# A linear attention on one core: queries kept as hi and lo halves in one tile, two phase passes for three

## The chip, the cores and the metric

The kernel runs on one core of one Trainium2 chip. The metric is the device time of one execution in microseconds (us). Three executions before the change took 1333.11, 1334.69 and 1338.66 us; their median, 1334.69 us, is the time before.

## The reference, cut to what matters

The program is one layer of a graph network over 1250 nodes of 1024 features: a first layer norm, a graph attention over 20000 edges, a linear attention, a feed-forward block and a quantised one. The change touches the linear attention alone:

```
p  = einsum('blhd,dm->blhm', x, proj_mat) / math.sqrt(D_HEAD)      # for queries and for keys
qp = kp = concatenate([cos(p), sin(p)], axis=-1) / math.sqrt(D_KMAP)
kv   = einsum('blhm,blhd->bhmd', kp, v)
attn = einsum('blhm,bhmd->blhd', qp, kv)
```

There are 16 heads of 64 features, and proj_mat is 64x128. The sines and cosines need phases p of nearly full float32 accuracy.

## The kernel before

TensorE works here on fp32r, a shortened float32. To keep accuracy every operand is split into hi (the value written as fp32r) and lo (the value less hi, again fp32r), and a product is three matmuls that add up in PSUM: lo times hi, hi times lo, hi times hi.

`linear_attention` takes two heads at a time, a pair: 8 pairs, a loop of 7 iterations and a last pair written out. The features of the pair lie on the 128 partitions (head 0 on 0 to 63, head 1 on 64 to 127) and the 1250 nodes along the columns, in three thirds of 418, 416 and 416 columns. A pair has, on TensorE (`block.tensor`, `pair`):

- products for values, keys and queries (`product`, L1414): three runs of 24 matmuls each, one run per third. ScalarE adds the bias and writes hi (`keep_run`, L1179); VectorE waits for that and writes lo (`keep_run`, L1306). Both read the product from PSUM.
- ten steps, k = 0 to 9. Steps 0 to 4 are for keys (`key_phases`, L1455, then `accumulate_kv`, L1477: six matmuls), steps 5 to 9 for queries, 250 nodes each (`query_phases`, L1465, then `attend`, L1489: twelve matmuls).

In every step the phases go from PSUM through three instructions of VectorE (`phases`: L1327 whole turns, L1329 the part of a turn, L1332 minus its absolute value, the only one of the three that reads SBUF alone), then through two sines and a copy to hi on ScalarE (`cos_sin`: L1201, L1203, L1214). The difference to lo is made by GpSimd in even steps (`keep_lo`, L1140) and by VectorE in odd ones (`keep_lo`, L1336). `accumulate_kv` and `attend` wait for that lo. The step buffers are double (k % 2).

The queries are held as q_hi and q_lo, each 128 partitions by 1250. proj_hi and proj_lo are 128 x 2 x 128: block h holds proj_mat in the 64 partitions of head h and zeros in the other 64, so that one matmul over all 128 partitions gives the phases of head h alone. Half of the array's rows multiply by zero.

The order on each engine is written out by hand in four functions called `pair`. What matters here is the order on the two elementwise engines, in which the query thirds stand first:

```
ScalarE: query third 0, weights' hi (keys), cos_sin 2, query third 1, weights' hi (values), cos_sin 3, query third 2, cos_sin 4, ...
VectorE: query third 0, keep_lo 1, phases 2, query third 1, phases 3, query third 2, keep_lo 3, phases 4, phases 5, ...
GpSimd:  keep_lo 0, weights' lo (keys), keep_lo 2, weights' lo (values), keep_lo 4, weights' lo (queries), keep_lo 6, keep_lo 8
TensorE: query run 0, accumulate 0, key phases 2, query run 1, accumulate 1, key phases 3, query run 2, accumulate 2, key phases 4,
         value run 0, accumulate 3, query phases 5, value run 1, accumulate 4, query phases 6, value run 2 with the transposes of kv, ...
```

The weights' hi and lo (L1171 on ScalarE, L1136 on GpSimd) are for the next pair, whose weights SyncE loads after it has issued the store of the pair before. The last pair has no next one: no value or key runs lie between its steps there, and ScalarE and VectorE split the weights of the following stage instead (L1221, L1340).

Of the kernel before, what the change touches and what calls it, by code (L numbers as in the profile page):

```python
# [5 lines left out]
ALU = mybir.AluOpType  # L6
ACT = mybir.ActivationFunctionType
AX = mybir.AxisListType
F32 = mybir.dt.float32
F32R = mybir.dt.float32r  # L10
# [5 lines left out]
N, D = 1250, 1024  # L16
# [10 lines left out]
HEADS, DH, KMAP = 16, 64, 128  # L27
# [13 lines left out]
def f32(ap):  # L41

    return ap.bitcast(F32)
# [933 lines left out]
VALUE, KEY, QUERY = 0, 1, 2  # L977
# [8 lines left out]
CHUNK = 2 * T  # L986
# [3 lines left out]
def linear_attention(core):  # L990
# [6 lines left out]
    with ExitStack() as ctx:  # L997
        def sb(name, shape, dt=F32):
            return ctx.enter_context(nc.sbuf_tensor(name, shape, dt))

        def ps(name, shape):
            return ctx.enter_context(nc.psum_tensor(name, shape, F32))
# [3 lines left out]
        bias = [core.cols[:, COLUMN_AT[f"L0_mix_b{n}"]] for n in "vkq"]  # L1006
        proj = sb("proj", [128, 2, KMAP])
        proj_hi = sb("proj_hi", [128, 2, KMAP], F32R)
        proj_lo = sb("proj_lo", [128, 2, KMAP], F32R)
        half_pi = sb("half_pi", [128, 1])  # L1010
        k_hi = sb("k_hi", [128, N], F32R)
        k_lo = sb("k_lo", [128, N], F32R)
        q_hi = sb("q_hi", [128, N], F32R)
        q_lo = sb("q_lo", [128, N], F32R)
        v_t = sb("v_t", [128, N])
        v_hi = sb("v_hi", [T, NT, 128], F32R)
        v_lo = sb("v_lo", [T, NT, 128], F32R)
# [10 lines left out]
        p_w = ps("p_w", [128, 3, 512])  # L1028
        p_p = ps("p_p", [128, 2, 512])
# [7 lines left out]
        s_prep = core.sem("projection_step")  # L1037
        s_prod = core.sem("third_product_done")
        s_kqhi = core.sem("key_or_query_hi_kept")
        s_klo = core.sem("keys_kept")  # L1040
        s_qlo = core.sem("queries_kept")
        s_vt = core.sem("values_kept")
# [22 lines left out]
        def done(j, k):  # L1065
            return 2 * STEPS * j + k + 1
# [31 lines left out]
        @block.sync  # L1098
        def _(sp):
            sp.wait_ge(s_zero, 1)  # L1100
            for h in range(2):
                sp.dma_start(proj[h * DH:(h + 1) * DH, h, :], inp["L0_mix_proj_mat"]).then_inc(s_proj, 16)

            for p in range(2):
                sp.wait_ge(core.counts_stored[p], MOVED * NT // 2)
                core.load_x(sp, p, p)

            def store(j):
                sp.wait_ge(s_atk, STEPS * j + STEPS)
                sp.dma_start(core.attn_dram[bass.ds(j * 128, 128), :], attn_t[:]).then_inc(s_st, 16)  # L1110

            with sp.Fori(0, PAIRS - 1) as j:
                for which in (KEY, VALUE, QUERY):
                    sp.wait_ge(s_wlo[which], j + 1)
                    core.load_mix(sp, which, j + 1)
                store(j)

            for k in range(K8):
                if k < 3:
                    sp.wait_ge(s_wlo[k], PAIRS)  # L1120
                else:
                    sp.wait_ge(s_gwlo, k - 2)
                sp.dma_start(gnn_w_in[k % 3][:].rearrange("p k n -> p (k n)"), inp["L0_gnn_W"][k * 128:(k + 1) * 128, :]
                             ).then_inc(s_gw[k % 3], 16)
            store(PAIRS - 1)

        @block.gpsimd
        def _(pool):
            pool.memset(proj[:], 0.0).then_inc(s_zero, 1)
            pool.memset(half_pi[:], HALF_PI).then_inc(s_zero, 1)  # L1130
            pool.memset(f32(kv_hi[:]), 0.0).then_inc(s_zero, 1)
            pool.memset(f32(kv_lo[:]), 0.0).then_inc(s_zero, 1)

            def split_lo(which, j):
                pool.wait_ge(s_whi[which], j + 1)
                pool.tensor_tensor(w_lo[which][:], w_in[which][:], f32(w_hi[which][:]), ALU.subtract).then_inc(s_wlo[which], 1)  # L1136

            def keep_lo(j, k):
                pool.wait_ge(s_cshi, done(j, k))
                pool.tensor_tensor(full(cs_lo, k), full(cs, k), f32(full(cs_hi, k)), ALU.subtract).then_inc(s_cslo[0], 1)  # L1140


            pool.wait_ge(s_proj, 32)
            pool.tensor_scalar(proj[:], proj[:], 1.0 / (DH ** 0.5 * 2 * 3.141592653589793), None, ALU.mult).then_inc(s_prep, 1)
            pool.wait_ge(s_prep, 1)
            pool.tensor_copy(proj_hi[:], proj[:]).then_inc(s_prep, 1)
            pool.wait_ge(s_prep, 2)
            pool.tensor_tensor(proj_lo[:], proj[:], f32(proj_hi[:]), ALU.subtract).then_inc(s_prep, 1)

            def pair(j, more):  # L1150
                keep_lo(j, 0)
                if more:
                    split_lo(KEY, j + 1)
                keep_lo(j, 2)
                if more:
                    split_lo(VALUE, j + 1)
                keep_lo(j, 4)
                if more:
                    split_lo(QUERY, j + 1)
                keep_lo(j, 6)  # L1160
                keep_lo(j, 8)

            with pool.Fori(0, PAIRS - 1) as j:
                pair(j, True)
            pair(PAIRS - 1, False)

        @block.scalar
        def _(act):
# [4 lines left out]
            def keep_run(which, j, n):  # L1173

                a, w = THIRDS[n]
                act.wait_ge(s_prod, 9 * j + 3 * which + n + 1)
                core.passed(act)
                out = (v_t, k_hi, q_hi)[which]
                act.activation(out[:, a:a + w], p_w[:, n, 0:w], ACT.Identity, bias=bias[which][:, bass.ds(j, 1)]  # L1179
                               ).then_inc(s_vt if which == VALUE else s_kqhi, 1)  # L1180

            def keep_v(j, group):

# [116 lines left out]
        def _(dve):  # L1300
            def keep_run(which, j, n):

                a, w = THIRDS[n]
                dve.wait_ge(s_kqhi, 6 * j + (3 if which == QUERY else 0) + n + 1)
                hi, lo, s = (k_hi, k_lo, s_klo) if which == KEY else (q_hi, q_lo, s_qlo)
                dve.scalar_tensor_tensor(lo[:, a:a + w], p_w[:, n, 0:w], bias[which][:, bass.ds(j, 1)], f32(hi[:, a:a + w]),  # L1306
                                         ALU.add, ALU.subtract).then_inc(s, 1)

            def keep_v(j, group):
                first, count = V_GROUPS[group]  # L1310
# [95 lines left out]
        def _(pe):  # L1406
# [52 lines left out]
            def query_phases(j, k):  # L1459
                c = k - STEPS  # L1460
                pe.wait_ge(s_qlo, 3 * j + (CHUNK * (c + 1) - 1) // 417 + 1)
                slot_free(pe, s_part, j, k)
                for h in range(2):
                    for m, (left, right) in enumerate(((proj_lo, q_hi), (proj_hi, q_lo), (proj_hi, q_hi))):
                        last = pe.matmul(p_p[:, k % 2, h * CHUNK:(h + 1) * CHUNK], left[:, h, :], right[:, c * CHUNK:(c + 1) * CHUNK],  # L1465
                                         start=(m == 0), stop=(m == 2))
                last.then_inc(s_p, 1)

            def accumulate_kv(j, k):
# [26 lines left out]
                key_run(0, n)  # L1496
            for group in range(3):
                transpose_v(0, group)
            pe.wait_ge(s_prep, 3)
            key_phases(0, 0)  # L1500
            key_phases(0, 1)

# [931 lines left out]
```

## Time and profile before

| what | value |
| --- | --- |
| median of three executions | 1334.69 us |
| the profiled execution's own time | 1334.61 us |
| its span, first to last instruction | 1332.8 us |
| TensorE busy with matmuls | 1247.7 us (94%), 7017 matmuls |
| VectorE busy | 766.2 us (57%) |
| ScalarE busy | 631.6 us (47%) |
| GpSimd busy | 340.5 us (26%) |
| mean granted TensorE clock | 0.971 |

The linear attention runs from about 157 to 709 us of the span. Busy time is the sum of the durations on an engine; idle time matters only on an engine that others wait for. Matmuls overlap in their pipeline, so what one costs is the distance between two starts and not its duration. The same is true, less strongly, of the elementwise engines.

### The profile page before, as it was taken

Reading aid. Unit: us, or ns where it says so; the run is one execution under the profiler, and the core shown is the slowest. Engines: PE = TensorE matmul, PEld = TensorE weight load, DVE = VectorE, ACT = ScalarE, POOL = GpSimd, SP = SyncE. Lnnn points to the kernel's source line nnn. Section 1 sums busy time; section 2 is a strip of 40 time slices with the busy share of each in tenths; the row PEclk is TensorE's granted clock in tenths of the full one; section 3 lists DMA queues with packets and bytes.
Section 4 is the critical chain, followed back from the end, with each engine's and each line's share of the span. In section 5 each row is a group of like instructions: output and inputs, shape, how many; then the busy total and the mean of one; then the engine's idle time right before and its main releaser. Section 6 shows DMA issues by size and latency. Waiting matters only on the chain. (4 is left out here: it accounts for less than half of the span.)

```text
span 1332.8 us, 19542 instructions
## 1 busy us (share of the span) xinstructions
PE 1247.7 (94%) x7017; PEld 1088.1 (82%) x7017; DVE 766.2 (57%) x1212; ACT 631.6 (47%) x917; POOL 340.5 (26%) x296
## 2 busy tenths in 40 slices
PE   6989889999999999999957999799999999899997
PEld 4556689999999999999946787699997887788874
DVE  7979625455655556565553376577774321556546
ACT  8175534555555555555554533332233442455544
POOL 1400003241423232332220201056662433021000
PEclk9999999999999999999976999899999799999999
DMA  8011310111020202020214645432335232620112
GB/s 207 10 29 25 78 36 1 33 35 54 12 66 0 66 0 66 0 66 0 67 45 150 216 151 172 137 107 81 92 91 192 74 93 62 211 72 14 50 32 93
DMA packets 72193, 99.41 MB, mean 75 GB/s; under 512 B 27241, under 2 KB 52165, under 8 KB 71631
## 3 DMA queue, kind: packets, MB, share of 16 engines
q1 hardware_dynamic: 68684, 86.11, 22.5%
q0 software_dynamic: 3456, 12.58, 3.1%
q8 instruction: 34, 0.56, 0.2%
q14 instruction: 19, 0.16, 0.0%
HBM read 77.04 MB, written 21.63 MB: 74 GB/s over the span
## 5 line engine op out<-in xcount | busy, mean ns | idle before, releaser
L1140 POOL TENSOR_TENSOR cos_sin_lo<-cos_sin,cos_sin_hi 125x1024 fp32r<-125x1024 f32 (+1 forms) x40 | 95.8, 2396 | 351.2 <-ACT cos_sin_hi L1214 351.2
L1201 ACT ACTIVATE cos_sin<-part_turn 125x512 f32<-125x512 f32 (+1 forms) x80 | 50.1, 627 | 152.7 <-DVE part_turn L1329 152.7
L468 PE MATMUL p_cnt<-hot_s,hot_d 125*125 125x418 bf16 x540 | 113.8, 361 | 1.8 <-DVE hot_d L401 1.8
L705 PE MATMUL p_h<-x 128*125 128x512 f32 x400 | 109.3, 400 | 0.0
L399 DVE TENSOR_SCALAR hot_s<-iota_h,ends 125x1250 bf16<-125x1250 f16 x180 | 98.2, 546 | 14.6 <-PE p_cnt L468 12.5
L468 PEld LDWEIGHTS p_cnt<-hot_s,hot_d 125*125 125x125 bf16 x540 | 63.3, 140 | 51.6 <-DVE hot_d L401 40.6
L1414 PE MATMUL p_w<-x,mix_hi_v 128*128 128x416 f32 (+1 forms) x384 | 105.2, 355 | 0.0
L1414 PE MATMUL p_w<-x,mix_hi_k 128*128 128x416 f32 (+1 forms) x384 | 104.2, 352 | 0.0
L1414 PE MATMUL p_w<-x,mix_hi_q 128*128 128x416 f32 (+1 forms) x384 | 104.1, 352 | 0.0
L966 PE MATMUL rows_in_psum<-h_hi,a_lo 125*125 125x342 f32 x300 | 96.8, 323 | 3.0 <-DVE a_lo L910 3.0
L1327 DVE TENSOR_SCALAR whole_turns<-p_p 125x512 f32<-125x512 f32 (+1 forms) x80 | 54.4, 680 | 77.0 <-PE p_p L1465 74.4
L966 PE MATMUL rows_in_psum<-h_lo,a_hi 125*125 125x342 f32 x300 | 96.7, 322 | 0.0
L966 PE MATMUL rows_in_psum<-h_hi,a_hi 125*125 125x342 f32 x300 | 96.5, 322 | 0.0
L705 PEld LDWEIGHTS p_h<-x 128*125 128x125 f32 x400 | 74.7, 188 | 18.0
L1214 ACT ACTIVATE cos_sin_hi<-cos_sin 125x1024 fp32r<-125x1024 f32 (+1 forms) x80 | 84.0, 1050 | 5.3
L1332 DVE SCALAR_TENSOR_TENSOR whole_turns<-part_turn 125x512 f32<-125x512 f32 (+1 forms) x80 | 80.9, 1011 | 2.7
L1744 PE MATMUL rows_in_psum<-wo_rest,at_hi 128*125 128x512 f32 x280 | 77.5, 399 | 0.0
L1414 PEld LDWEIGHTS p_w<-x,mix_hi_v 128*128 128x128 f32 x384 | 73.1, 191 | 0.8
L1414 PEld LDWEIGHTS p_w<-x,mix_hi_q 128*128 128x128 f32 x384 | 72.2, 188 | 0.9
L1414 PEld LDWEIGHTS p_w<-x,mix_hi_k 128*128 128x128 f32 x384 | 72.3, 188 | 0.7
L1414 PE MATMUL p_w<-x,mix_lo_v 128*128 128x416 f32 (+1 forms) x192 | 68.8, 358 | 3.5 <-PEq L134 3.5
L1203 ACT ACTIVATE cos_sin<-whole_turns,half_pi 125x512 f32<-125x512 f32 (+1 forms) x80 | 57.5, 718 | 30.1 <-DVE whole_turns L1332 25.3
(302 smaller groups left out, 3169.8 us busy)
## 6 DMA issues: line engine op xcount, KB each, us to landing
x_in<-in_x_dram SPq DMA_DIRECT2D x30, 448.0 KB
attn_dram<-attn_t SPq DMA_DIRECT2D x8, 625.0 KB, 3.9
at_in<-attn_dram SPq DMA_DIRECT2D x10, 500.0 KB, 4.6
x_rows<-in_x_dram SPq DMA_DIRECT2D x10, 448.0 KB
x_in<-gnn_dram SPq DMA_DIRECT2D x10, 448.0 KB
out_dram<-rows SPq DMA_DIRECT2D x10, 448.0 KB
mix_in_v<-in_L_mix_wv_dram SPq DMA_DIRECT2D x8, 512.0 KB, 6.0
mix_in_k<-in_L_mix_wk_dram SPq DMA_DIRECT2D x8, 512.0 KB, 4.7
```

Source lines behind the costliest of these rows:

```text
L399: dve.tensor_scalar(hot_s[:, j, :], iota_h[:], ends[:, at, 0:1].rearrange("p a b -> p (a b)"), None, ALU.is_equal)
L468: last = pe.matmul(p_cnt[0:T, t % 2, n, 0:w], hot_d[:, j, 0:T], hot_s[:, j, a:a + w], start=False, stop=False)
L705: last = pe.matmul(p_h[0:T, i % 2, n, :], left[i % 2][:, k, :], right[:, k, cols], start=(k == 0 and m == 0), stop=(k == K8 - 1 and m == 2))
L966: last = pe.matmul(p_o[0:T, i % 2, n, 0:H_COLS], left[:, i % 2, d, :], right[:, d, cols], start=(d == 0 and m == 0), stop=(d == NT - 1 and ...
L1140: pool.tensor_tensor(full(cs_lo, k), full(cs, k), f32(full(cs_hi, k)), ALU.subtract).then_inc(s_cslo[0], 1)
L1201: act.activation(step_view(cs, k, 1), rows(part, k), ACT.Sin, scale=TWO_PI)
L1203: act.activation(step_view(cs, k, 0), rows(away, k), ACT.Sin, scale=TWO_PI, bias=half_pi[0:T if k < STEPS else 128, :]).then_inc(s_cs, 1)
L1214: act.activation(full(cs_hi, k), full(cs, k), ACT.Copy).then_inc(s_cshi, 1)
L1327: dve.tensor_scalar(flat(whole, k), flat(p_p, k), MAGIC, -MAGIC, ALU.add, ALU.add).then_inc(s_whole, 1)
L1332: dve.scalar_tensor_tensor(flat(away, k), flat(part, k), -1.0, flat(part, k), ALU.mult, ALU.min).then_inc(s_away, 1)
L1414: last = pe.matmul(p_w[:, n, 0:w], left[which][:, k, :], right[:, k, a:a + w], start=(k == 0 and m == 0), stop=(k == K8 - 1 and m == 2))
L1744: last = pe.matmul(p_o[i % 2][0:T, n, :], left[i % 2][:, k, :], right[:, n * 512:(n + 1) * 512], start=(k == 0 and m == 0), stop=(k == K8 ...
```

## The change

A new tile q_both (128 x 2 x 1250) takes the place of q_hi and q_lo. Its plane h holds head h alone: hi in the head's own 64 partitions, lo in the other 64. A new tile proj_both holds proj_lo in both halves (plane 0) and proj_hi in both halves (plane 1), made once by two additions on GpSimd. A pass over all 128 partitions then gives proj times (hi + lo) of one head, so two matmuls per head and step do what three did; they also add the product lo times lo that was left out before. ScalarE and VectorE write each query third in two instructions of 64 partitions where there was one of 128; VectorE's write goes to the other head's partitions.

```diff
-        q_hi = sb("q_hi", [128, N], F32R)
-        q_lo = sb("q_lo", [128, N], F32R)
+        q_both = sb("q_both", [128, 2, N], F32R)
+        proj_both = sb("proj_both", [128, 2, KMAP], F32R)
...
+            pool.wait_ge(s_prep, 3)
+            for n, half in enumerate((proj_lo, proj_hi)):
+                pool.tensor_tensor(proj_both[:, n], f32(half[:, 0]), f32(half[:, 1]), ALU.add).then_inc(s_prep, 1)
...
-                out = (v_t, k_hi, q_hi)[which]
-                act.activation(out[:, a:a + w], p_w[:, n, 0:w], ACT.Identity, bias=bias[which][:, bass.ds(j, 1)]
-                               ).then_inc(s_vt if which == VALUE else s_kqhi, 1)
+                if which == QUERY:
+                    for h in range(2):
+                        head = slice(h * DH, (h + 1) * DH)
+                        last = act.activation(q_both[head, h, a:a + w], p_w[head, n, 0:w], ACT.Identity, bias=bias[which][head, bass.ds(j, 1)])
+                    last.then_inc(s_kqhi, 1)
...
+                if which == QUERY:
+                    for h in range(2):
+                        head, other = slice(h * DH, (h + 1) * DH), slice((1 - h) * DH, (2 - h) * DH)
+                        last = dve.scalar_tensor_tensor(q_both[other, h, a:a + w], p_w[head, n, 0:w], bias[which][head, bass.ds(j, 1)],
+                                                        f32(q_both[head, h, a:a + w]), ALU.add, ALU.subtract)
+                    last.then_inc(s_qlo, 1)
...
-                    for m, (left, right) in enumerate(((proj_lo, q_hi), (proj_hi, q_lo), (proj_hi, q_hi))):
-                        last = pe.matmul(p_p[:, k % 2, h * CHUNK:(h + 1) * CHUNK], left[:, h, :], right[:, c * CHUNK:(c + 1) * CHUNK],
-                                         start=(m == 0), stop=(m == 2))
+                    for m in range(2):
+                        last = pe.matmul(p_p[:, k % 2, h * CHUNK:(h + 1) * CHUNK], proj_both[:, m], q_both[:, h, c * CHUNK:(c + 1) * CHUNK],
+                                         start=(m == 0), stop=(m == 1))
...
-            pe.wait_ge(s_prep, 3)
+            pe.wait_ge(s_prep, 5)
```

Values and keys are kept as before.

## Rows read from the trace of the kernel before

**Rows 1.** Page, part 1: engine, busy us (share of the span), instructions.
```profile
PE 1247.7 (94%) x7017; PEld 1088.1 (82%) x7017; DVE 766.2 (57%) x1212; ACT 631.6 (47%) x917; POOL 340.5 (26%) x296
```
**Rows 2.** Windows of pairs 2 and 7: length, then busy time per engine (instructions), clock.
```profile
324.05:388.40 64.35, 63.83 (x382) 61.69 (x381) 36.91 (x47) 34.86 (x53) 19.50 (x8) 1.00 0.13 34
...
645.80:709.30 63.50, 43.11 (x216) 39.48 (x214) 36.76 (x47) 34.53 (x49) 12.47 (x5) 0.82 0.26 86
```
**Rows 3.** TensorE's waits from 185 to 735 us: total us, times, longest.
```profile
PE p_at L1489 <- ACT attn_t L1225: 7.9, 3, 4.2
PE p_tr L1446 <- DVE kv_t L1345: 6.5, 8, 2.8
```
**Rows 4.** The query phases: one of their three forms, and two neighbours by start.
```profile
L1465 PE MATMUL p_p<-q_lo,proj_hi x80: 273/278/415, 221.4 to 696.5; 128*128 128x250 f32 x80
...
350.34 0.28 PE L1465 MATMUL p_p<-q_hi,proj_lo 128*128 128x250 f32 x1
350.45 0.28 PE L1465 MATMUL p_p<-q_lo,proj_hi 128*128 128x250 f32 x1
```
**Rows 5.** ScalarE in pair 2: start us, duration us, instruction, idle before.
```profile
331.86 1.06 ACT L1171 ACTIVATE mix_hi_k<-mix_in_k 128x1024 fp32r<-128x1024 f32 x1 [1.02 <-DMA mix_in_k<-in_L_mix_wk_dram]
...
337.70 0.59 ACT L1179 ACTIVATE q_hi<-p_w,columns 128x416 fp32r<-128x416 f32 x1
338.19 1.05 ACT L1171 ACTIVATE mix_hi_v<-mix_in_v 128x1024 fp32r<-128x1024 f32 x1
```
**Rows 6.** VectorE in pair 2.
```profile
331.57 1.21 DVE L1336 TENSOR_TENSOR cos_sin_lo<-cos_sin,cos_sin_hi 125x1024 fp32r<-125x1024 f32 x1
...
334.15 1.80 DVE L1332 SCALAR_TENSOR_TENSOR whole_turns<-part_turn 125x512 f32<-125x512 f32 x1
...
340.34 2.85 DVE L1332 SCALAR_TENSOR_TENSOR whole_turns<-part_turn 125x512 f32<-125x512 f32 x1
...
345.64 0.65 DVE L1306 SCALAR_TENSOR_TENSOR q_lo<-p_w,columns,q_hi 128x416 fp32r<-128x416 f32 x1 [2.46 <-ACT q_hi L1179]
346.21 1.22 DVE L1336 TENSOR_TENSOR cos_sin_lo<-cos_sin,cos_sin_hi 125x1024 fp32r<-125x1024 f32 x1
```
**Rows 7.** TensorE in pair 2: the first matmul of accumulate 3 and of 4.
```profile
348.61 0.40 PE L1477 MATMUL p_kv<-cos_sin_hi,v_lo 125*128 125x512 f32 x1
...
355.24 0.40 PE L1477 MATMUL p_kv<-cos_sin_hi,v_lo 125*128 125x512 f32 x1
```
**Rows 8.** GpSimd in pair 2.
```profile
333.00 2.40 POOL L1136 TENSOR_TENSOR mix_lo_k<-mix_in_k,mix_hi_k 128x1024 fp32r<-128x1024 f32 x1 [5.25 <-ACT mix_hi_k L1171]
337.88 2.41 POOL L1140 TENSOR_TENSOR cos_sin_lo<-cos_sin,cos_sin_hi 125x1024 fp32r<-125x1024 f32 x1 [2.48 <-ACT cos_sin_hi L1214]
340.23 2.40 POOL L1136 TENSOR_TENSOR mix_lo_v<-mix_in_v,mix_hi_v 128x1024 fp32r<-128x1024 f32 x1
...
351.48 2.41 POOL L1140 TENSOR_TENSOR cos_sin_lo<-cos_sin,cos_sin_hi 125x1024 fp32r<-125x1024 f32 x1 [8.85 <-ACT cos_sin_hi L1214]
```
**Rows 9.** VectorE and GpSimd side by side in pair 0.
```profile
199.25 1.22 DVE L1336 TENSOR_TENSOR cos_sin_lo<-cos_sin,cos_sin_hi 125x1024 fp32r<-125x1024 f32 x1
199.54 3.15 POOL L1136 TENSOR_TENSOR mix_lo_k<-mix_in_k,mix_hi_k 128x1024 fp32r<-128x1024 f32 x1 [1.30 <-ACT mix_hi_k L1171]
```
**Rows 10.** Pair 1, where the keys' weights land later.
```profile
269.33 1.06 ACT L1171 ACTIVATE mix_hi_k<-mix_in_k 128x1024 fp32r<-128x1024 f32 x1 [2.84 <-DMA mix_in_k<-in_L_mix_wk_dram]
...
269.79 0.69 DVE L1332 SCALAR_TENSOR_TENSOR whole_turns<-part_turn 125x512 f32<-125x512 f32 x1
...
270.47 2.41 POOL L1136 TENSOR_TENSOR mix_lo_k<-mix_in_k,mix_hi_k 128x1024 fp32r<-128x1024 f32 x1 [7.08 <-ACT mix_hi_k L1171]
```
**Rows 11.** Pair 7: ScalarE's last query third, TensorE's accumulate 3 and 4.
```profile
664.01 0.61 ACT L1179 ACTIVATE q_hi<-p_w,columns 128x416 fp32r<-128x416 f32 x1 [0.60 <-PE p_w L1414]
...
666.59 0.47 PE L1477 MATMUL p_kv<-cos_sin_hi,v_lo 125*128 125x512 f32 x1 [0.61 <-DVE cos_sin_lo L1336]
...
673.40 0.76 PE L1477 MATMUL p_kv<-cos_sin_hi,v_lo 125*128 125x512 f32 x1 [4.49 <-POOL cos_sin_lo L1140]
```

More of the change, by code:

```diff
@@ L1177, in keep_run @@
                 core.passed(act)
-                out = (v_t, k_hi, q_hi)[which]
-                act.activation(out[:, a:a + w], p_w[:, n, 0:w], ACT.Identity, bias=bias[which][:, bass.ds(j, 1)]
-                               ).then_inc(s_vt if which == VALUE else s_kqhi, 1)
+                if which == QUERY:
[3 more added lines that the diff above has]
+                    last.then_inc(s_kqhi, 1)
+                else:
+                    out = (v_t, k_hi)[which]
+                    act.activation(out[:, a:a + w], p_w[:, n, 0:w], ACT.Identity, bias=bias[which][:, bass.ds(j, 1)]
+                                   ).then_inc(s_vt if which == VALUE else s_kqhi, 1)
             def keep_v(j, group):
@@ L1304, in keep_run @@
                 dve.wait_ge(s_kqhi, 6 * j + (3 if which == QUERY else 0) + n + 1)
-                hi, lo, s = (k_hi, k_lo, s_klo) if which == KEY else (q_hi, q_lo, s_qlo)
-                dve.scalar_tensor_tensor(lo[:, a:a + w], p_w[:, n, 0:w], bias[which][:, bass.ds(j, 1)], f32(hi[:, a:a + w]),
-                                         ALU.add, ALU.subtract).then_inc(s, 1)
+                if which == QUERY:
[4 more added lines that the diff above has]
+                    last.then_inc(s_qlo, 1)
+                else:
+                    dve.scalar_tensor_tensor(k_lo[:, a:a + w], p_w[:, n, 0:w], bias[which][:, bass.ds(j, 1)], f32(k_hi[:, a:a + w]),
+                                             ALU.add, ALU.subtract).then_inc(s_klo, 1)
             def keep_v(j, group):
```

## The prediction

> **What bounds the kernel now.** I read the shares of busy time first: TensorE has 94% of the span, no other engine over 57% [rows 1]. Then the busy time by pair: in pair 2 TensorE is busy 63.83 of 64.35 us at clock 1.00, in pair 7, the last, 43.11 of 63.50 us at 0.82 [rows 2]. So in the loop a matmul less is a gain as long as no wait comes in its place; in pair 7 it is not, since TensorE stands there for others. The waits name them: the transposes of kv wait for VectorE's copy once in every pair (6.5 us in 8, the longest 2.8, so 0.53 in each of the others), and attend waits for attn_t on ScalarE three times, 7.9 us, all in pair 7 [rows 3]. Last I read pairs 0, 1, 2 and 7 engine by engine. That decides the case: the averages say that VectorE and ScalarE are half idle, the order in time says how close behind them TensorE follows.
>
> **What is removed.** A query step loses two of six matmuls. Each of three forms occurs 80 times [rows 4], 240 matmuls become 160, the rest is untouched, so 7017 should become 6937. The price is the distance of two starts, 0.11 to 0.12 us (350.34 to 350.45) [rows 4], not the 0.28 of duration. I take 0.118: 80 x 0.118 = 9.4 us, 0.24 a step, 1.18 a pair. The vacated pass frees nobody else.
>
> **What is added once.** Two additions and a wait on GpSimd, and TensorE's wait for them (s_prep 5 for 3). They lie beside TensorE's six value and key runs, 144 matmuls ahead of the first step, and GpSimd has nothing to do there until its first keep_lo, so I take nothing; with that cover gone it would be under 2 x 2.40 us once, the price of two of its instructions of 1024 columns [rows 8], where these have 128.
>
> **What is added in each third.** ScalarE and VectorE each run two instructions over the same 416 columns where one ran. Start to start the present ones take 0.49 us on ScalarE (337.70 to 338.19) [rows 5] and 0.57 us on VectorE (345.64 to 346.21) [rows 6]. No row shows one of 64 partitions. Upper bound, nothing overlapping: the durations, 0.59 + 0.65 = 1.24. Lower bound, if time went by elements: two halves cost what the whole did, 0 added; a gain is excluded, since no half does more than half the work in less than half the time. I take 1.06, since every partition works by itself and its columns stay. VectorE waits for the second hi (one semaphore), so both add up behind one another: whatever follows the query third on VectorE is 1.06 us late, on ScalarE 0.49.
>
> The Trainium skill (VectorE: DVE Perf Modes, the section on the TRN2 errata) prices an instruction that reads PSUM by a fixed part and its columns: 120 + 416 cycles at 0.96 GHz on VectorE, 172 + 416 at 1.2 GHz on ScalarE, an estimate of 0.56 + 0.49 = 1.05 us, with no term for partitions. It speaks against the low end; the sum by it is the one by the rows.
>
> **Pair 2, step by step.** Behind query third 0 on VectorE stand keep_lo 1 and phases 2; behind it on ScalarE the weights' hi, which waits 1.02 us for its DMA [rows 5] and so covers ScalarE's 0.49. VectorE's 1.06 does this: keep_lo 1 moves from 331.57 to 332.63 and ends at 333.84 [rows 6]. GpSimd's weights' lo starts at 333.00 [rows 8], now inside it. Pair 0 shows what that costs: GpSimd began at 199.54 while keep_lo 1 ran until 200.47, and took 3.15 us for 2.40 [rows 9]: 0.75 for an overlap of 0.93, that is the overlap less 0.18. Here: 0.84 - 0.18 = 0.66, the weights' lo ends at 336.06 for 335.40.
>
> L1332 of step 2 (334.15, now 335.21) stood behind that instruction before: it took 1.80 us for the usual 0.69 and ended 0.55 after GpSimd [rows 6, 8]. So its own 1.06 is swallowed and it is late by 0.66 only. ScalarE's cosine, its copy to hi, GpSimd's keep_lo 2 and the values' weights' lo follow with 0.66. Third 1 adds 1.06 again, and again L1332 of step 3 is swallowed: it starts at 340.34, stands behind GpSimd until 342.63 and ends at 343.19 [rows 6, 8]; now 343.85. Third 2 has no such cover. keep_lo 3 moves from 346.21 by 0.66 + 1.06 to 347.93 and ends at 349.15; accumulate 3 wanted to start at 348.61 [rows 7]. It had 1.13 us to spare (1.18, less 0.05 for the signal; from ScalarE's 332.92 to GpSimd's 333.00 it is 0.08 [rows 5, 8]), it needs 1.72: a new wait of 0.59. GpSimd's keep_lo 4 (351.48 to 353.89) [rows 8] ends at 355.61, and accumulate 4 would now start at 355.24 + 0.59 - 0.24 = 355.59 [rows 7]: another 0.08. From step 5 on VectorE follows TensorE's query phases, and all moves with them; the wait for kv_t stays.
>
> So pair 2 gives 1.18 - 0.67 = 0.51. Pairs 3 to 6 are copies: 5 x 0.51 = 2.5 us.
>
> The Trainium skill (SBUF — State Buffer, Who interferes with whom) has VectorE instructions with two SBUF inputs and GpSimd ones that read SBUF exclude each other, the later one blocked for the whole instruction of the first. By "whole" the 0.66 would be 0.84 and the sum 0.9 us later; the pair 0 rows decide for 0.66.
>
> **Pair 1.** Its weights land late: ScalarE waits 2.84 us until 269.33, GpSimd's lo starts at 270.47, and L1332 of step 2 got in ahead of it at 269.79 [rows 10]. With 1.06 more it starts at 270.85, after GpSimd, and stands until 270.47 + 2.41 + 0.55 = 273.43. Pair 2's old place, one period of 64.35 us earlier, is 335.95 - 64.35 = 271.60; so this pair is 1.83 behind it. Then 1.83 + 1.06 - 1.13 + 0.08 = 1.84 us of new waits at accumulate 2 to 4: it loses 0.66 net.
>
> **Pair 0** waits at its start and has its steps well ahead after that; I take the whole 1.18.
>
> **Pair 7** has no split of weights on GpSimd in its steps, so no cover: the three thirds add up, 3.18, less the 0.60 us that ScalarE stood idle before third 2; accumulate 3 waited already (0.61), accumulate 4 too (4.49) [rows 11]. TensorE is 2.5 late there. Query phases 6 and 7 give back 0.24 and about 0.47 (at the lower clock); after that ScalarE leads (the waits for attn_t) [rows 3] and phases 8 and 9 give nothing. Net 1.8 lost, and the next stage starts as much later.
>
> **Sum.** -1.18 + 0.66 - 2.5 + 1.8 = -1.2 us on the profiled execution's 1334.61 (a span of 1332.8 and 1.8 around it); the median is 0.08 above it: **1333.5 us**. The ends of the third's price: with 0 nothing is late anywhere, 7 x 1.18 and 0.7 in pair 7 are saved, 9.0: 1325.7. With 1.24, pairs 2 to 6 wait 1.03, pair 1 2.02, pair 7 loses 2.4: -1.18 + 0.84 - 0.75 + 2.4 = +1.3, 1336.0.
>
> **Rivals.**
> A, everything fits: all new work disappears in idle time. For it: VectorE's 57%. Against it: 1.13 us of room at accumulate 3 for 1.72. 7 x 1.18 = 8.3, pair 7 even: 1326.4.
> B, the two engines miss each other: the weights land a little later, or keep_lo 1 gets out in time, and the 0.66 is gone. For it: the landing differs from pair to pair [rows 5, 10]. Then pairs 2 to 6 need 1.06 of 1.13 and save all, 5.9: -1.18 + 0.66 - 5.9 + 1.8 = -4.6, 1330.1.
> C, slower: nothing is swallowed. If L1332 no longer ends by GpSimd's release but by its own chain, as in pair 7, the three thirds add up: 3.18 + 0.66 - 1.13 + 0.08 = 2.8 of waits a pair, 1.6 net in pairs 1 to 6: 9.6 + 1.8 - 1.2 = +10.2, 1344.9. It decides against the change once a loop pair's delay passes 1.13 + 1.18 = 2.3 us. Against it: the 1.80 and 2.85 us of L1332 [rows 6].
> That the matmuls don't go is excluded by their count.
>
> **How the numbers follow.** Forecast 0.45, A 0.20, B 0.22, C 0.08, the rest (more than one at once, the clock in pair 7) 0.05. Three runs spread by 5.5 us, and about 0.5% (6.7 us) is what this kernel's measurement tells from no change. Faster by over that means under 1328.0: most of A, 0.17. Slower means over 1341.4: most of C, 0.06. Between them 0.77. The range goes from the low end to somewhat beyond the high end of the third's price, 1325.7 to 1337.5, and leaves out C and part of the rest.
>
> **What would show it.** Right: 6937 matmuls; q_hi's place at 48 instructions of about 0.59 us and VectorE's at 48 of 0.65; in pairs 2 to 6 a wait of TensorE for keep_lo on VectorE at L1477, 0.6 each; GpSimd's weights' lo for the keys at about 3.0 us; pair lengths of 63.8 us (pair 1: 65.0); the last pair longer by 1.8. Wrong: loop pairs of 63.2 without a wait (A, or B if pair 1 and 7 still lose), or of 65.9 (C); half instructions well under 0.5 us; a wait of TensorE at another line, first of all at L1465 for the queries, which I hold for free since third 2 is needed by query phases 8 only.

## The result, and the profile after

The changed kernel takes 1347.44 us, the median of five executions (1343.09 to 1349.66), against 1334.68 us for the kernel before (five, 1333.11 to 1338.66). The ratio is 1.0092, with a 95% interval of 1.0065 to 1.0118: slower by 12.8 us, where 1.2 us faster was forecast, and outside the range.

The page's part 1 answers to [rows 1]. The 80 matmuls are gone, and TensorE's busy time has not fallen; VectorE and ScalarE have 24 instructions more each.
```profile
PE 1248.0 (93%) x6937; PEld 1083.3 (80%) x6937; DVE 774.2 (57%) x1236; ACT 647.4 (48%) x941; POOL 341.1 (25%) x298
```
The windows of two loop pairs, 2 and 4, and of pair 7, columns as in [rows 2]. The loop pairs are cut here from accumulate 0 to the next accumulate 0 (in [rows 2] from the query run; a period has the same length either way), pair 7 from accumulate 0 to the first transpose of the next stage, which before was 61.46.
```profile
332.53:399.13 66.60, 63.34 (x372) 60.36 (x371) 37.46 (x50) 36.91 (x56) 19.09 (x8) 1.00 0.12 33
465.73:530.73 65.00, 63.01 (x372) 60.32 (x371) 35.89 (x50) 36.90 (x56) 19.65 (x8) 1.00 0.13 34
660.77:725.38 64.61, 38.12 (x182) 34.17 (x180) 38.31 (x46) 35.22 (x49) 10.37 (x5) 0.76 0.23 78
```
Here is the first thing to see: by their length the loop has two kinds of pairs. Pair 0 and pairs 1, 4, 5 and 6 take 65.0 to 65.1 us (before 65.99 and 64.35), pairs 2 and 3 take 66.6. TensorE's waits from 185 to 760 us answer to [rows 3]: the wait for kv_t is what it was, attend's is 8.6 for 7.9, and the wait for the keys' lo on VectorE (L1493) now stands on top:
```profile
PE p_kv L1493 <- DVE cos_sin_lo L1352: 17.4, 10, 4.5
PE p_at L1505 <- ACT attn_t L1235: 8.6, 3, 4.1
PE p_tr L1462 <- DVE kv_t L1361: 6.5, 8, 2.8
```
In the kernel before, from 185 to 735 us, that wait had 0.6 us, in pair 7 (the one for the lo on GpSimd, 6.3, has fallen to 2.9):
```profile
PE p_kv L1477 <- POOL cos_sin_lo L1140: 6.3, 2, 4.5
...
PE p_kv L1477 <- DVE cos_sin_lo L1336: 0.6, 1, 0.6
```
The instructions that write q_both (duration least/median/most in ns, first and last start): a half over 64 partitions lasts as long as the whole did (0.59 and 0.65 us in [rows 5, 6]).
```profile
L1481 PE MATMUL p_p<-q_both,proj_both x160: 273/280/415, 225.5 to 709.5; 128*128 128x250 f32 x160
L1185 ACT ACTIVATE q_both<-p_w,columns x48: 587/603/607, 202.8 to 677.5; 64x416 fp32r<-64x416 f32 x32, 64x418 fp32r<-64x418 f32 x16
L1318 DVE SCALAR_TENSOR_TENSOR q_both<-p_w,columns,q_both x48: 644/652/658, 204.2 to 678.8; 64x416 fp32r<-64x416 f32 x32, 64x418 fp32r<-64x418 f32 x16
```
VectorE in pair 4 (start us, duration us; x2 is the two halves together), with accumulate 0 at 465.73:
```profile
468.71 1.32 DVE L1318 SCALAR_TENSOR_TENSOR q_both<-p_w,columns,q_both 64x418 fp32r<-64x418 f32 x2 [3.12 <-ACT q_both L1185]
470.06 1.23 DVE L1352 TENSOR_TENSOR cos_sin_lo<-cos_sin,cos_sin_hi 125x1024 fp32r<-125x1024 f32 x1
471.32 0.69 DVE L1343 TENSOR_SCALAR whole_turns<-p_p 125x512 f32<-125x512 f32 x1
...
472.77 1.33 DVE L1348 SCALAR_TENSOR_TENSOR whole_turns<-part_turn 125x512 f32<-125x512 f32 x1
...
480.02 1.32 DVE L1348 SCALAR_TENSOR_TENSOR whole_turns<-part_turn 125x512 f32<-125x512 f32 x1
484.55 1.31 DVE L1318 SCALAR_TENSOR_TENSOR q_both<-p_w,columns,q_both 64x416 fp32r<-64x416 f32 x2 [3.21 <-ACT q_both L1185]
485.89 1.22 DVE L1352 TENSOR_TENSOR cos_sin_lo<-cos_sin,cos_sin_hi 125x1024 fp32r<-125x1024 f32 x1
```
ScalarE, GpSimd and TensorE in the same pair:
```profile
474.89 1.06 ACT L1224 ACTIVATE cos_sin_hi<-cos_sin 125x1024 fp32r<-125x1024 f32 x1
475.98 1.22 ACT L1185 ACTIVATE q_both<-p_w,columns 64x416 fp32r<-64x416 f32 x2
477.22 1.06 ACT L1175 ACTIVATE mix_hi_v<-mix_in_v 128x1024 fp32r<-128x1024 f32 x1
```
```profile
470.59 2.96 POOL L1137 TENSOR_TENSOR mix_lo_k<-mix_in_k,mix_hi_k 128x1024 fp32r<-128x1024 f32 x1 [5.75 <-ACT mix_hi_k L1175]
```
```profile
487.26 0.47 PE L1493 MATMUL p_kv<-cos_sin_hi,v_lo 125*128 125x512 f32 x1 [1.46 <-DVE cos_sin_lo L1352]
```
Two halves keep VectorE 1.34 us (484.55 to 485.89) where one instruction kept it 0.57, and ScalarE 1.24 (475.98 to 477.22) for 0.49. keep_lo 3 starts 20.16 us after accumulate 0; before it was 17.57 (346.21 [rows 6] less 328.64, its accumulate 0). It is 2.59 late, and accumulate 3, which waits for it, stands 1.46.

Pair 2 is the other kind (accumulate 0 at 332.53). GpSimd's weights' lo starts 0.03 us ahead of VectorE's keep_lo 1, which then takes 3.45 us instead of 1.23, and TensorE waits at accumulate 1 as well:
```profile
336.83 2.39 POOL L1137 TENSOR_TENSOR mix_lo_k<-mix_in_k,mix_hi_k 128x1024 fp32r<-128x1024 f32 x1 [5.18 <-ACT mix_hi_k L1175]
336.86 3.45 DVE L1352 TENSOR_TENSOR cos_sin_lo<-cos_sin,cos_sin_hi 125x1024 fp32r<-125x1024 f32 x1
...
340.45 0.47 PE L1493 MATMUL p_kv<-cos_sin_hi,v_lo 125*128 125x512 f32 x1 [1.14 <-DVE cos_sin_lo L1352]
```
In pair 5 keep_lo 1 starts 0.05 us ahead. It takes its usual time, GpSimd takes 3.45 us for 2.40, and the pair is one of 65.0:
```profile
535.06 1.23 DVE L1352 TENSOR_TENSOR cos_sin_lo<-cos_sin,cos_sin_hi 125x1024 fp32r<-125x1024 f32 x1
```
```profile
535.11 3.45 POOL L1137 TENSOR_TENSOR mix_lo_k<-mix_in_k,mix_hi_k 128x1024 fp32r<-128x1024 f32 x1 [5.26 <-ACT mix_hi_k L1175]
```
The profiled executions differ by 14.6 us (1349.20 less 1334.61). The loop's seven pairs, from 452.1 to 458.4, are 6.25 of it: 65.08 for 65.99 in pair 0, about +0.67 in each of pairs 1, 4, 5 and 6, and +2.25 in each of pairs 2 and 3. Pair 7 is 3.15 (61.46 to 64.61). Accumulate 0 of pair 0 comes 4.1 later, and about 1.1 comes after pair 7.

The 4.1 belong to this execution and not to the change. The windows of the attention's start, here in the changed kernel:
```profile
159.02:202.42 43.40, 40.44 (x190) 39.43 (x191) 10.05 (x14) 11.02 (x16) 6.53 (x10) 0.85 0.29 67
```
and in a second profiled execution of the same kernel (r_after below), where it takes what it took before (41.36 us at 0.96):
```profile
157.04:198.42 41.38, 36.62 (x191) 35.44 (x191) 9.99 (x14) 11.28 (x17) 6.47 (x10) 0.96 0.28 70
```
The granted clock, a mean over the levels 1.2 and 2.4 GHz, is 0.85 in one and 0.96 in the other. In the 98 us ahead of it, which the change doesn't touch, it was 0.94 in the first and 0.98 in the kernel before. The profiled execution of e_late_before below, which has no part of the change, reaches accumulate 0 as late (202.86). What lowered the clock is open.

### The profile page after: what moved, and what is told of

The parts are those of the page before. It is cut to its first block and busy times, and to the rows that moved or that the text cites. A ratio compares the mean times of both kernels' runs of the same rounds, so it can differ in the third digit from the quotient of the medians.

```text
span 1347.4 us, 19446 instructions
## 1 busy us (share of the span) xinstructions
PE 1248.0 (93%) x6937; PEld 1083.3 (80%) x6937; DVE 774.2 (57%) x1236; ACT 647.4 (48%) x941; POOL 341.1 (25%) x298
## 5 line engine op out<-in xcount | busy, mean ns | idle before, releaser
L1343 DVE TENSOR_SCALAR whole_turns<-p_p 125x512 f32<-125x512 f32 (+1 forms) x80 | 54.6, 683 | 63.3 <-PE p_p L1481 61.8
L1318 DVE SCALAR_TENSOR_TENSOR q_both<-p_w,columns,q_both 64x416 fp32r<-64x416 f32 (+1 forms) x48 | 31.2, 651 | 77.0 <-ACT q_both L1185 76.6
L1430 PE MATMUL p_w<-x,mix_lo_q 128*128 128x416 f32 (+1 forms) x192 | 68.1, 355 | 0.0
```

The lines of the kernel that those rows point to most:

```text
L1343: dve.tensor_scalar(flat(whole, k), flat(p_p, k), MAGIC, -MAGIC, ALU.add, ALU.add).then_inc(s_whole, 1)
L1430: last = pe.matmul(p_w[:, n, 0:w], left[which][:, k, :], right[:, k, a:a + w], start=(k == 0 and m == 0), stop=(k == K8 - 1 and m == 2))
```

## The experiments

Theory T at the outset: the price of two halves is not that of two instructions in a row; the overlap with the neighbours is lost, and the 1.5 us a third push keep_lo 3 past its room (the time it can be late before TensorE waits for it). Rival R: the price is as forecast, and what costs is the collision with GpSimd, above all in pairs of the second kind. A third question was whether TensorE's two passes save what was taken for them.

**m_parts**, a kernel by itself: eight instructions in a row of one kind, 416 columns from PSUM, on ScalarE and on VectorE. Partitions 0 to 127 (full), 0 to 63 (low), 0 to 63 and 64 to 127 by turns (alt), the same written to the other half (cross), 128 and 64 partitions by turns (mix). It computes nothing of the reference and writes zeros.

```
for n, (a, b) in enumerate(pattern):      # (read, write) partitions
    act.activation(tiles["act", name][b, n, :], pa[a, 0:W], ACT.Identity, bias=bias[a, :])
    dve.scalar_tensor_tensor(tiles["dve", name][b, n, :], pd[a, 0:W], bias[a, :], src[a, :], ALU.add, ALU.subtract)
```


> A kernel of its own that computes nothing of the reference (it writes zeros): groups of 8 instructions over 416 columns from PSUM, on ScalarE (activation with a bias column) and on VectorE (scalar_tensor_tensor as for q_lo). In each group the partitions differ: 'full' always 128; 'low' always 0 to 63; 'alt' 0 to 63 and 64 to 127 in turn; 'cross' as alt but written to the other half (VectorE alone); 'mix' 128 and 0 to 63 in turn; 'copy' as alt without the bias column (ScalarE alone). Theory 1 (the halves of the changed kernel don't overlap because two neighbours cover different partitions): start to start 0.49 us on ScalarE and 0.57 on VectorE for full and for low, 0.60 to 0.65 for alt, cross and mix. Rival (any two instructions without a wait between them, or any 64-partition ones, stand 0.60 and 0.66 apart, whatever they cover): low as alt, and perhaps full as alt too. Rival (writing across partitions costs): cross slower than alt on VectorE.

ScalarE, then VectorE; the second number is the time of all eight.
```profile
3.25 4.09 ACT L93 ACTIVATE act_full<-p_act,bias_col 128x416 fp32r<-128x416 f32 x8 [1.24 <-DVE p_dve L102]
7.18 4.92 ACT L93 ACTIVATE act_alt<-p_act,bias_col 64x416 fp32r<-64x416 f32 x8
12.11 4.05 ACT L93 ACTIVATE act_low<-p_act,bias_col 64x416 fp32r<-64x416 f32 x8
16.04 4.07 ACT L93 ACTIVATE act_mix<-p_act,bias_col 128x416 fp32r<-128x416 f32 x8
```
```profile
3.25 4.56 DVE L106 SCALAR_TENSOR_TENSOR dve_full<-p_dve,bias_col,src_tile 128x416 fp32r<-128x416 f32 x8
7.73 5.29 DVE L106 SCALAR_TENSOR_TENSOR dve_alt<-p_dve,bias_col,src_tile 64x416 fp32r<-64x416 f32 x8
13.04 4.56 DVE L106 SCALAR_TENSOR_TENSOR dve_low<-p_dve,bias_col,src_tile 64x416 fp32r<-64x416 f32 x8
17.61 5.30 DVE L106 SCALAR_TENSOR_TENSOR dve_cross<-p_dve,bias_col,src_tile 64x416 fp32r<-64x416 f32 x8
22.92 4.55 DVE L106 SCALAR_TENSOR_TENSOR dve_mix<-p_dve,bias_col,src_tile 128x416 fp32r<-128x416 f32 x8
```
Less one duration (0.60, 0.65) and by seven, the distance of two starts is 0.50 us on ScalarE for full, low and mix and 0.62 for alt; on VectorE 0.56 and 0.66. So 64 partitions cost what 128 do, writing across costs nothing (cross is alt), and each change of the first partition between 0 and 64 costs the overlap, 0.12 and 0.10 us. The part of T that mix too would lose it was wrong: mix has the 0.50 and 0.56 of full. The last group, alt on ScalarE without the bias column, took 4.22 us for eight of 0.51: 0.53 from start to start, so the instructions don't overlap there either, though there was no group beside it that kept to one partition. The Trainium skill (VectorE: DVE Perf Modes, its TRN2 errata) prices one instruction by a fixed part and its columns; the equal times of full and low agree with it.

**r_after**, the changed kernel once more beside the other two parts.

> The changed kernel again, beside the kernel before on the same chip. If the loss is of the program and not of the day: 1343 to 1350 us, some 12 above before, and again a larger spread than before. In the profile the pairs of the loop are either 65.0 or 66.6 us long (before 64.35), and which of the two goes with whether GpSimd's weights' lo for the keys starts before or after VectorE's keep_lo 1.

1343.62 us (1340.49 to 1347.88), ratio 1.0068 (1.0045 to 1.0091). Its profiled execution, 1342.14, has no pair of 66.6: 64.82, 65.36, and five of 65.02 to 65.04; pair 7 64.57. In pairs 1 to 6 keep_lo 1 comes first. In pair 0 GpSimd does, by 0.35 us (200.42 and 200.77, as in the first profile, 205.19 and 205.54), and keep_lo 1 takes 3.11, but accumulate 1 doesn't wait for it there. So the slowdown is there without the longer pairs. The difference of its profile from the first (7.1 us) is 3.0 in the pairs and 4.0 before accumulate 0.

**e_split**, the halves alone on the kernel before: q_hi and q_lo stay, three passes stay.
```diff
-                act.activation(out[:, a:a + w], p_w[:, n, 0:w], ACT.Identity, bias=...)
+                    for h in range(2):
+                        last = act.activation(q_hi[head, a:a + w], p_w[head, n, 0:w], ACT.Identity, bias=...)
...
+                for part_ in parts:
+                    last = dve.scalar_tensor_tensor(lo[part_, a:a + w], p_w[part_, n, 0:w], ..., f32(hi[part_, a:a + w]), ...)
```


> The kernel before, its three passes kept, with the query thirds written in two instructions of 64 partitions each on ScalarE and VectorE (q_hi, q_lo, own partitions): the split's cost alone. Theory 1 (the split delays keep_lo 3 by 2.7 us, TensorE waits 1.5 at accumulate 3 in each loop pair, 4 more in the last): the waits of the changed kernel without its 0.24 us a step, so pairs of 66.2 or 67.8 us, in all 18 to 24 us above before, 1353 to 1359. Rival (the split is covered as the forecast had it, and what costs is the new tile's layout, in the passes or in the write across partitions): within 4 us of before.

**e_passes**, two passes alone on the kernel before; the product proj_lo times q_hi is left out, so its phases are short of it.
```diff
-                    for m, (left, right) in enumerate(((proj_lo, q_hi), (proj_hi, q_lo), (proj_hi, q_hi))):
+                    for m, (left, right) in enumerate(((proj_hi, q_lo), (proj_hi, q_hi))):
```


> The kernel before with the pass proj_lo times q_hi left out of the query phases and all else as it was (the phases lack that term): the gain of the passes alone. Theory 1: 1.18 us less in each loop pair (63.2 us), the last pair 0.5 less or nothing, 8.3 to 9 us below before, 1326. Rival (the passes give nothing since the loop is bound by the chain of the other engines): within 2 us of before, with new waits at accumulate or at the transposes of kv.

The halves alone: 1354.53 us (1350.82 to 1356.40), ratio 1.0132 (1.0110 to 1.0153). The passes alone: 1326.99 (1324.34 to 1329.28), 0.9935 (0.9915 to 0.9954). A pair of the first kind and one of the second of e_split, then a pair of e_passes:
```profile
397.32:463.54 66.22, 64.28 (x382) 61.53 (x381) 35.90 (x50) 37.02 (x56) 20.17 (x8) 1.00 0.13 33
529.75:597.58 67.83, 64.62 (x382) 61.52 (x380) 37.48 (x50) 37.02 (x56) 19.34 (x8) 1.00 0.12 33
```
```profile
387.06:450.23 63.17, 62.65 (x371) 60.49 (x370) 36.90 (x47) 34.76 (x53) 19.50 (x8) 1.00 0.13 35
```
On 64.35 us the halves put 1.87 and the passes take 1.18: +0.69 together, and the changed kernel has +0.65. The ratios multiply to 1.0066, beside the 1.0068 of r_after. The two parts add up; the gain in a loop pair is as forecast and all there, and the loss is the halves' alone.

**e_dvefirst** forces the first kind: GpSimd's weights' lo for the keys waits for VectorE's keep_lo 1.
```diff
+                    pool.wait_ge(s_cslo[1], lo_done(j, 1))
                     split_lo(KEY, j + 1)
```


> The changed kernel with one more wait on GpSimd: its weights' lo for the keys starts only after VectorE's keep_lo 1. Theory (the pairs of 66.6 us are those in which GpSimd came first and VectorE's keep_lo 1 stood behind it): no pair over 65.4 us in the profile, no wait at accumulate 1; the best runs as before (1340 to 1343), the slow end of the spread gone or nearly so. Rival (the two lengths come from the weights' landing itself or from the clock): 66.6 us pairs and waits at accumulate 1 still occur.

**e_poolfirst** forces the second: keep_lo 1 waits for GpSimd.
```diff
+                if more:
+                    dve.wait_ge(s_wlo[KEY], j + 2)
                 keep_lo(j, 1)
```


> The changed kernel with one more wait on VectorE: keep_lo 1 starts only after GpSimd's weights' lo for the keys, in pairs 0 to 6. Theory: every loop pair is at least 66.6 us long, pair 1 (whose weights land 1 to 2 us later) longer, a wait of 1.2 us or more at accumulate 1 each time: 1352 to 1357. Rival (the order of the two doesn't matter, as the delay is swallowed later): within 2 us of the changed kernel.

e_dvefirst: 1342.96 us (1341.02 to 1347.47), ratio 1.0062 (1.0042 to 1.0082); no wait at accumulate 1, pair 0 63.45, pair 1 65.73 (over the 65.4 expected), loop pairs from the third on 65.3. e_poolfirst: 1353.99 (1352.89 to 1357.74), 1.0146 (1.0122 to 1.0171); pair 0 64.93 (under the 66.6 expected), pair 1 68.35, pairs from the third on 66.9 to 67.4. TensorE's wait in it, from 206 to 655 us:
```profile
PE p_kv L1495 <- DVE cos_sin_lo L1352: 19.0, 11, 2.9
```
So the order of the two is worth 1.5 to 2.1 us a pair, 11 us in all; but with it forced the good way nearly all of the slowdown remains. That refutes R. The second kind explains pairs 2 and 3 of the first profile (2 x 1.6 of 14.6 us); that the number of such pairs also makes the spread of the other executions was not shown, since they have no profile, and it can't be all of it: with the good order forced one of six executions still took 1347.47.

**e_halfsig** changes how the halves follow one another: ScalarE signals each half, and VectorE starts its first after ScalarE's first.
```diff
-                    last.then_inc(s_kqhi, 1)
+                        act.activation(q_both[head, h, a:a + w], ...).then_inc(s_kqhi, 1)
...
+                        dve.wait_ge(s_kqhi, 9 * j + 3 + 2 * n + h + 1)
```


> The changed kernel with ScalarE's two halves signalled one by one, so that VectorE's first half starts behind ScalarE's first and not behind its second. Theory (what costs is that the two pairs of halves stand one behind the other, 1.24 + 1.33 us to keep_lo where 0.62 + 0.57 stood): 0.6 us less of delay at each third, 0.6 once and once more in the wait at accumulate 3, which shrinks from 1.46 to 0.3 or less; pairs of about 63.9 us, in all 8 to 10 below the changed kernel, 1333 to 1336, about the time before. Rival (the ScalarE part of the delay is not on the path, VectorE's halves alone decide): less than 3 us gained.

1332.57 us (1329.80 to 1336.24), ratio 0.9979 (0.9964 to 0.9994): 14.9 us under the changed kernel's first median, 11.1 under r_after's, for 8 to 10 expected; between the profiled executions of r_after and this run it is 9.0. Loop pairs from the third on take 63.8. VectorE's idle time before a third falls from 3.12 to 2.50 us (pair 3, accumulate 0 at 391.23), keep_lo 1 comes 0.62 earlier and keep_lo 3 (410.17) is 18.94 behind accumulate 0 instead of 20.16. Two of the three steps of 0.6 count, because the one in between is swallowed by GpSimd, as L1348's 1.94 us show:
```profile
393.59 1.32 DVE L1320 SCALAR_TENSOR_TENSOR q_both<-p_w,columns,q_both 64x418 fp32r<-64x418 f32 x2 [2.50 <-ACT q_both L1185]
...
404.30 1.94 DVE L1350 SCALAR_TENSOR_TENSOR whole_turns<-part_turn 125x512 f32<-125x512 f32 x1
...
410.17 1.23 DVE L1354 TENSOR_TENSOR cos_sin_lo<-cos_sin,cos_sin_hi 125x1024 fp32r<-125x1024 f32 x1
```
**e_lofirst** changes what stands behind the halves: on VectorE keep_lo 1 goes ahead of third 0, keep_lo 3 ahead of third 2. **e_lofirst_before** is the same order on the kernel before.
```diff
+                keep_lo(j, 1)
                 keep_run(QUERY, j, 0)
-                keep_lo(j, 1)
...
+                keep_lo(j, 3)
                 keep_run(QUERY, j, 2)
-                keep_lo(j, 3)
```


> The changed kernel with VectorE's keep_lo 1 ahead of query third 0 and its keep_lo 3 ahead of query third 2. Theory (TensorE waits at accumulate 1 and 3 only because the query thirds, which it needs 8 us later at the earliest, stand in front of these two): no wait at accumulate 1 or 3 in the loop, pairs of 63.2 us, the last pair within 2 us of before: 1326 to 1328. Rival (the delay goes on through phases and cosines and comes out at the next wait, accumulate 4 or the transposes of kv): pairs over 64 us, 1333 or more.

> The kernel before, with the same two moves on VectorE as in the run before (keep_lo 1 ahead of query third 0, keep_lo 3 ahead of query third 2), without the change: what the order alone is worth. Theory (the kernel before has no wait at accumulate in the loop, one of 0.6 us in the last pair): pairs of 64.35 us as before, 1333 to 1336, no difference. So the gain of the reordered changed kernel is the two passes' own. Rival (the order itself gives much of the 9 us): 1330 or less.

1326.39 us (1325.91 to 1329.22), ratio 0.9939 (0.9922 to 0.9956); loop pairs 63.12 to 63.28, pair 7 62.62. On the kernel before the order does nothing: 1333.93 (1331.61 to 1341.88), 1.0000 (0.9985 to 1.0014), pairs 64.35. The halves cost as much as ever, but nothing that TensorE needs stands behind them.

**e_late** goes further, for pair 7: every third goes one step later than its phases (keep_lo 1, phases 2, third 0, phases 3, third 1, keep_lo 3, phases 4, third 2). **e_late_half** adds the signals of e_halfsig, **e_late_before** is the order on the kernel before.
```diff
+                keep_lo(j, 1)
+                phases(j, 2)
                 keep_run(QUERY, j, 0)
-                keep_lo(j, 1)
-                phases(j, 2)
+                phases(j, 3)
                 keep_run(QUERY, j, 1)
-                phases(j, 3)
+                keep_lo(j, 3)
+                phases(j, 4)
                 keep_run(QUERY, j, 2)
-                keep_lo(j, 3)
-                phases(j, 4)
```


> The changed kernel with the query thirds on VectorE moved further back: keep_lo 1, phases 2, third 0, phases 3, third 1, keep_lo 3, phases 4, third 2. Theory: in the loop nothing more to gain than with the two keep_lo alone (pairs of 63.1 us, there is no wait left but the one for kv_t); in the last pair phases 2 to 4 no longer stand behind a third, so TensorE's waits at accumulate 4 (5.7 us) and after shrink by 1.2 to 2: 1324 to 1326, 1 to 2 below e_lofirst. Rival (the last pair is bound by ScalarE's thirds, which are where they were): same as e_lofirst.

> e_late with ScalarE's halves signalled one by one as in e_halfsig. Theory: VectorE's thirds are off TensorE's path now, so this gives nothing in the loop and at most 0.5 us in the last pair: the same as e_late within 0.5 us. Rival: 2 us or more.

> The kernel before with VectorE's order as in e_late: again what order alone is worth. Theory: the loop pairs stay at 64.35 us, the last pair gains 0.5 to 1.5 us: 1333 to 1335, so e_late is 8 to 9 us below it, the whole of the passes' gain (9.4 us of starts).

e_late 1324.78 us (1321.25 to 1330.38), ratio 0.9928 (0.9904 to 0.9952); e_late_half 1323.87 (1321.83 to 1324.67), 0.9915 (0.9898 to 0.9932); e_late_before 1334.61 (1333.62 to 1340.78), 1.0010 (0.9994 to 1.0026). e_late's pair 3, and all of TensorE's waits in its loop from 206 to 655 us:
```profile
388.83:451.96 63.13, 62.60 (x371) 60.52 (x370) 37.69 (x50) 36.92 (x56) 19.01 (x8) 1.00 0.13 35
```
```profile
PE p_tr L1462 <- DVE kv_t L1361: 3.7, 7, 0.5
```
Pair 7 takes 60.25 us, 1.2 less than before. In e_late_before it takes 61.90: there the order was expected to gain 0.5 to 1.5 us, and it gains nothing. e_late_half beats both kernels, the one before by 0.85%, the changed one by 1.75% (0.9915 over 1.0092; 1.5% by r_after's 1.0068); its 0.9 us under e_late are within the spread, so the half signals are worth nothing shown once the order is right.

## Why the prediction was wrong, step by step

**What held.** TensorE bounds, and a matmul less is a gain where no wait replaces it: 6937 matmuls; 1.18 a pair forecast, 1.18 in e_passes (64.35 to 63.17), 1.22 in e_late. The two additions at the start cost nothing that shows. The wait for kv_t stayed (6.5 us in 8). L1332 of steps 2 and 3 (now L1348) still ends by GpSimd's release: 1.33 and 1.32 us for its usual 0.69, where 1.80 and 2.85 stood before [rows 6]. GpSimd's weights' lo did collide with keep_lo 1, at about the price read from pair 0: 0.56 for an overlap of 0.70 (470.59 to keep_lo 1's end, 471.29), the overlap less 0.14 where the forecast took it less 0.18.

**The step that failed: the third's price.** Forecast 1.06, at most 1.24. Measured by pair 4's rows: third 0 makes VectorE 1.40 late (0.62 for the second half on ScalarE, 0.78 on VectorE), thirds 1 and 2 each 1.53 (0.12 more, which ScalarE loses ahead of its first half: from 474.89 to 475.98 it is 1.09, before 0.96). The bound was no bound. It priced the added instruction at its full duration, 0.59 and 0.65, and kept for the one that was there the start-to-start 0.49 and 0.57, which holds overlap with its neighbours. m_parts shows that this overlap goes too: two changes of partition a third, 0.12 and 0.10 each. With no overlap at all the same durations give 2 x (0.59 + 0.65) for the 0.49 + 0.57 of before, 1.42 more, beside the 1.40 of third 0.

The 0.12 ahead of thirds 1 and 2 shows something further. The instruction in front, cos_sin_hi, reads and writes SBUF from partition 0, so the neighbours don't differ; but the last one to read PSUM was the second half of the third before, from partition 64. Ahead of third 0 it was attn_t, from partition 0, and nothing is lost (466.38 to 467.35). VectorE has the same behind keep_lo 1, which reads SBUF alone: L1343, the next to read PSUM, starts 1.26 us after it in pair 4 (470.06 to 471.32), and 1.13 before (331.57 [rows 6] to 332.70). ScalarE's 0.96 of before is 336.74 to 337.70 [rows 5]:
```profile
332.70 0.68 DVE L1327 TENSOR_SCALAR whole_turns<-p_p 125x512 f32<-125x512 f32 x1
```
```profile
336.74 1.06 ACT L1214 ACTIVATE cos_sin_hi<-cos_sin 125x1024 fp32r<-125x1024 f32 x1
```
That the last read of PSUM decides fits all of these rows; no run changed it by itself.

**The walk of a pair was right, with that size in it.** keep_lo 1 is 1.40 late and so is its end; GpSimd's end, tied to it, is 1.06 late (473.55 less 465.73 is 7.82, against 6.76 before [rows 8]) where 0.66 was forecast, and third 2 adds 1.53: 2.59 for the 1.72 forecast. The room was 1.13, which leaves the 1.46 of the wait. In TensorE's starts it is somewhat more: against e_late accumulate 3 is 1.62 later, and by the end of accumulate 4 it is 1.87 (the forecast had 0.08 for accumulate 4); what makes up the 0.33 beyond 1.46 + 0.08 was not found. -1.22 + 1.87 = +0.65, where -1.18 + 0.67 = -0.51 was forecast. The point that decides was named, 2.3 us of delay; the pair went past it.

**The second kind of pair** was not in the prediction. It has keep_lo 1 first and GpSimd second, as in all the rows of before, and put GpSimd's start at 0.37 behind the moved keep_lo 1 (333.00 and 332.63). With 0.34 more the two starts fall together, and the landing of the weights decides: ahead of the weights' hi ScalarE stood idle 0.34 us in pairs 2 and 3, and 0.42 to 0.90 in pairs 1, 4, 5 and 6. Where GpSimd wins, keep_lo 1 is late until GpSimd's end and the pair takes 66.60: two pairs, 2 x 1.6 us. The Trainium skill (SBUF — State Buffer, Who interferes with whom) has the later of the two blocked for the whole instruction of the first, in either order. keep_lo 1's 3.45 us agree but for 0.14: they are 2.22 more than 1.23, and GpSimd ran 2.36 beside it.

**Pair 7**: 1.8 forecast, 3.15 measured. Accumulate 4 is 26.51 us behind accumulate 0 (687.28 less 660.77; before 23.00, 673.40 [rows 11] less 650.40): 3.5 late for 2.5, three thirds at the larger price. (At accumulate 3 it is 3.87, from 16.19 to 20.06 behind accumulate 0, and 1.40 + 2 x 1.53 less ScalarE's 0.60 is 3.86.) Of it 0.36 came back and not 0.7. **Pair 0** gained 0.91 of 1.18 in the first profile and 1.17 in the second. The second has the conditions that the forecast took: TensorE runs a part of the pair's first 8.3 us at 1.2 GHz (0.79 in the mean, as in the kernel before), and the other engines get well ahead. The first profile's 0.91 is luck, since there that stretch ran at full clock, and the slow one lay ahead of accumulate 0 (0.73 from 190.00 to 202.42). The kernel before, then the changed one:
```profile
198.30:206.59 8.29, 8.29 (x36) 7.68 (x37) 3.86 (x5) 3.59 (x5) 3.33 (x2) 0.79 0.00 0
```
```profile
202.42:209.06 6.64, 6.64 (x37) 6.34 (x37) 4.80 (x4) 2.27 (x3) 2.39 (x1) 1.00 0.00 1
```
It gave 1.65 us, and a wait of 1.5 at accumulate 3 took most of it: at full clock pair 0 takes the 65.0 to 65.1 of the other pairs.

**Pair 1** lost 0.68 and 1.01 for 0.66 forecast: close, and partly by chance, since in the first run its weights didn't land late. ScalarE stood idle 0.89 us ahead of their hi, as in pair 4 (0.90), where it was 2.84 before [rows 10] and 1.77 in the second.

**The rivals.** A and B had the mechanism of a third that fits; it didn't. C came nearest in time, 1344.9 for 1347.44, and by its threshold, but not by its reason: L1332 stayed swallowed. The forecast failed on a bound taken too narrow, and the range with it. With 1.53 for the last third, and GpSimd's end 1.06 late, the same walk gives 1.54 of waits and 0.36 net in pairs 2 to 6, and 1.83 + 1.53 - 1.13 + 0.08 = 2.31 and 1.13 net in pair 1; with pair 7 as measured that is -1.18 + 1.13 + 5 x 0.36 + 3.15 = +4.9 us. TensorE's later restart, 0.3 in each of five pairs, makes it 6.4, where the second profile has 6.3 (3.2 in the pairs, 3.1 in pair 7), and two pairs of the second kind make it 9.6, where the first has 9.4 (with pair 0 and pair 1 each some way off). The clock ahead of accumulate 0 is the rest of the first profile's difference but for 1.1.

## What to carry to other kernels

Price a split of one elementwise instruction by what its engine does between the neighbours' starts, before and after, not by the added piece alone: two halves with different first partitions cost 1.22 and 1.33 us here for 0.49 and 0.57. Where an operation grows that others stand behind on its engine, look first at what the bounding engine waits for next and put that ahead of it: the order alone turned +0.9% (+0.7% in the second measurement) into -0.7%, and did nothing for the kernel before.

## What was not expected of the hardware

ScalarE and VectorE overlap the end of an instruction with the start of the next by about 0.10 us (416 columns from PSUM: 0.50 and 0.56 from start to start, durations 0.60 and 0.65), and they don't where the first partition changes between 0 and 64 (0.62 and 0.66). The number of partitions and a write to the other half change nothing. The loss also shows at a distance, at the next instruction that reads PSUM, with instructions over SBUF alone in between (ScalarE 1.09 us for 0.96, VectorE 1.26 for 1.13).

When VectorE's and GpSimd's instructions over SBUF operands fall together, a few hundredths of a microsecond decide which of them goes first: GpSimd where it started 0.03 us ahead, VectorE where it started 0.05 ahead, and it shifts a pair by 1.6 us.
